# Graph attention on one core: turning probability blocks and adding edge masks as two halves of 64 rows, with both masks of pairs 1 and 2 laid by ScalarE

## Chip, cores and metric

The kernel runs on one core of a Trainium2 chip. The metric is the device time of one execution in microseconds (us), the median of several. A single profiled execution gives the rows shown below; times in rows are counted from the start of its span.

## What is computed

One layer over 1250 nodes with 512 features and 8 heads of 64. The part that this change touches is attention over the edges of a graph: for each edge a score, a softmax over all edges of a node and head, and a weighted sum of values.

```python
scores = jnp.einsum('ehd,ehd->eh', q[origin], k[destination]) * SCALE
ws = scores * edge_weights                      # 41250 edges x 8 heads
seg_max = jax.ops.segment_max(ws, origin, num_segments=N)
e = jnp.exp(ws - seg_max[origin])
denom = jax.ops.segment_sum(e, origin, num_segments=N)
att = e / (denom[origin] + 1e-16)
values = jax.ops.segment_sum(att[:, :, None] * v[destination], origin, num_segments=N)
```

Ahead of it stand two normalisations, the projections, and a linear attention over the same rows; behind it an output projection, a residual, a normalisation and some bit arithmetic on 48 columns. None of these is changed.

## The kernel before

The edges are scattered into a dense table of 1250 rows by 1360 columns (nodes, and 110 extra columns for edges that occur twice), and attention is then computed densely: an empty cell gets a penalty of -BIG, so that its exponential is zero. The rows are cut into 10 tiles of 128 nodes (the last has 98), the columns into three groups of 512, 512 and 336. A **tile** w (0 to 29) is one row tile in one group: 0 to 9 are group 0, 10 to 19 group 1, 20 to 29 group 2. Its eight heads are four **pairs** 0 to 3, and `u = 4 w + pair` numbers the pairs through the program; `hh` is 0 or 1, the head in its pair. A **step** d (0 to 59) handles two pairs: an even step (`q == 0`) pairs 0 and 1, an odd one pairs 2 and 3. So a tile is two steps.

For each head of a step, in this order over the engines:

- TensorE, `scores(d)` (L1319): two heads of a pair at once, one in array rows 0 to 63 and one in rows 64 to 127, since a head has 64 features. Each f32 product is two instructions of 512 columns, so a step has 8.
- The mask. `mask(w)` on VectorE (L1728) makes the penalty `pen` of a tile once, in bf16, in the odd step of the tile before. It is then put into the bank of PSUM in one of two ways: either ScalarE copies it there before the scores, which then add to it (`lay_mask`, L920; the head is "laid"), or TensorE adds it behind the scores as a product with the identity `identb` (L1326, 128x128). The table `OVER_MASK` says which heads of a group are laid.
- VectorE, `weighted` (L1841): multiplies scores and edge weights, takes the running maximum, and writes `ws`; `shift_of` (L1855) negates the maximum.
- ScalarE, `exps` (L912): the exponential in place, two instructions for a pair.
- TensorE, `transposes(d - 1)` (L1342): turns each head's 128x512 into four blocks 128x128 in one bank. ScalarE (`probs`, L927) or VectorE (`odd_probs`, L1862) copies the bank to SBUF.
- TensorE, `values` (L1364): the products with V, 64 columns of the array a head.

Each engine has a fixed order written out as code. That of TensorE in step d is `scores(d)`, the mask additions of step d, `transposes(d - 1)`, `values` of step d - 2. Seven banks are used as a ring in the order of the list `USES`: a bank is free for its next use when its reader has counted up its semaphore. In an even step the last of the four banks that `transposes(d - 1)` writes, that of pair 3's second head, is the bank that `scores(d)` used for pair 0's first head, so `free` waits until VectorE has read that one.

ScalarE in an odd step copies turned blocks, then does

```python
for u, hh in lay_order(d):
    if hh == 0:
        lay_mask(u, hh)
if late:
    pairs(2 * d - 1)
exps(2 * d)
for u, hh in lay_order(d):
    if hh == 1:
        lay_mask(u, hh)
exps(2 * d + 1)
```

where `lay_order(d)` lists the laid heads of step d + 1, here pairs 0 and 1 of the next tile. `lay_mask` waits for that tile's `mask` and for the bank. VectorE in an odd step does `weighted` four times, then `mask(w + 1)`, in group 1 `rescaled(w - 1)` (L1887), a shift and the copies. In an even step it starts with `weighted` of pair 0. `scores` waits for both laid heads of a pair ahead of that pair.

Of the kernel before, what the change touches and what calls it, by code (L numbers as in the profile page):

```python
# [15 lines left out]
P = 128  # L16
NT = 10
# [28 lines left out]
GROUPS = ((0, 512), (512, 512), (1024, COLS - 1024))  # L46
# [5 lines left out]
ND = NU // 2  # L52
NB = 7
ODD_ON_ACT = ((2,), (1, 2), ())
OVER_MASK = (((3, 1), (1, 1), (2, 0), (2, 1)), ((3, 1), (1, 1), (2, 0), (2, 1)), ((2, 0), (2, 1), (3, 1), (0, 0), (1, 0)))
FIN = ((0, 8), (8, 2))


def rows_of(t):
    return LAST if t == NT - 1 else P  # L60
# [7 lines left out]
def blocks(g):  # L68

    d0, n = GROUPS[g]  # L70
    return ((0, P, 8), (P, LAST, 9), (N - d0, X, None)) if g == 2 else tuple((i * P, P, d0 // P + i) for i in range(4))
# [7 lines left out]
def laid(u, hh):  # L79

    return u > 5 and (u % 4, hh) in OVER_MASK[u // 4 // NT] and not partly_written(USE_OF["s", u, hh] - NB)


def partly_written(r):

    return USES[r][0] == "t" and rows_of(USES[r][1] // 4 % NT) < P
# [12 lines left out]
def four(d):  # L99

    return [(2 * d + i // 2, i % 2) for i in range(4)]


def emptied(k):
# [63 lines left out]
def gps_layer(nc, x, src, dst, w_edge, ln_g, ln_b, Wq, bq, Wk, bk, Wv, bv, W1, b1, W2, b2,  # L168
# [3 lines left out]
    with ctx:  # L172
# [5 lines left out]
        def sem(name):  # L178
            return ctx.enter_context(nc.semaphore(name))
# [20 lines left out]
        ident = sb("ident", [P, P])  # L200
        identb = sb("identb", [P, P], BF16)
# [41 lines left out]
        def ar(a, n, parts=P):  # L243
            return AR[0:parts, a:a + n]
# [61 lines left out]
        ws = [sets, sets, [tight[0], tight[1], sets[2], tight[2]]]  # L306
        KVx = [ar(10240 + 1024 * i, 1024) for i in range(3)]
        pen = [ar(14192 + 256 * i, 256).bitcast(BF16) for i in range(2)]
# [106 lines left out]
        s_s = [sem(f"scores_ready{i}") for i in range(4)]  # L415
        s_bk = [sem(f"bank_read{i}") for i in range(NB)]
        s_nm = sem("shift_ready")
        s_exp = sem("exp_ready")
        s_t = sem("probs_transposed")
        s_pv = sem("values_summed")  # L420
        s_vfa = sem("first_values_kept")
        s_vfd = sem("values_merged")
# [52 lines left out]
        def use(what):  # L475

            return bank[USE_OF[what] % NB][:, :]
# [11 lines left out]
        def free(eng, what):  # L489

            r = USE_OF[what]
            if r >= NB:
                eng.wait_ge(s_bk[r % NB], r // NB)
# [518 lines left out]
        def _(pe):  # L1012
            mm = nc.tensor.matmul
# [103 lines left out]
            for m in range(KC):  # L1117
                b = proj(("w1t", m))
                for i in range(KC):
                    last = nc.tensor.transpose(b[:, i * P:(i + 1) * P], sW1[:, i, m * P:(m + 1) * P], ident[:, :])  # L1120
# [15 lines left out]
            for m in range(KC):  # L1136
                last = mm(b[:, m:m + 1], ball[:, m * P:(m + 1) * P], fourth[:, 0:1], start=True, stop=True)
# [101 lines left out]
            for k in range(KC):  # L1239
                last = nc.tensor.transpose(b[:, k * P:(k + 1) * P], kvBD[:, k, :], ident[:, :])  # L1240
# [59 lines left out]
            def scores(d):  # L1300
                w, q = d // 2, d % 2
                g, c = w // NT, w % NT
                d0, n = GROUPS[g]
                if g == 2 and q == 0:
                    gone(pe, ("l", w))
                for p in (2 * q, 2 * q + 1):
                    u = 4 * w + p
                    over = [laid(u, hh) for hh in range(2)]
                    bs = [use(("s", u, hh)) for hh in range(2)]
                    qs = [QT[64 * hh:64 * hh + 64, p, c * P:(c + 1) * P] for hh in range(2)]  # L1310
                    if u in (1, 2):
                        banks_left((2 * u - 2, 2 * u - 1))
                    for hh in range(2):
                        if over[hh]:
                            pe.wait_ge(s_laid, LAID_OF[u, hh] + 1)
                        else:
                            free(pe, ("s", u, hh))
                    for hh in range(2):
                        last = mm(bs[hh][:, 0:n], qs[hh], KT[64 * hh:64 * hh + 64, p, d0:d0 + n], start=not over[hh], stop=over[hh], skip_group_check=over[hh])  # L1319
                        if over[hh]:  # L1320
                            last.then_inc(s_s[2 * (p % 2) + hh], 1)
                if q == 0:
                    pe.wait_ge(s_pen, w + 1)
                for i, (u, hh) in enumerate(four(d)):
                    if not laid(u, hh):
                        mm(use(("s", u, hh))[:, 0:n], identb[:, :], pen[w % 2][:, 0:n], start=False, stop=True).then_inc(s_s[i], 1)  # L1326

            def last_mix():
                r = rows_of(NT - 1)
# [3 lines left out]
                last.then_inc(s_ly, 1)  # L1333

            def transposes(d):
                g, r = d // 2 // NT, rows_of(d // 2 % NT)
                for u, hh in four(d):
                    pe.wait_ge(s_exp, 2 * u + hh + 1)
                    free(pe, ("t", u, hh))
                    bl = blocks(g)  # L1340
                    for i, (a, rws, _) in enumerate(bl):
                        last = mm(use(("t", u, hh))[0:rws, i * P:i * P + r], ws[g][u % 4][hh][0:r, a:a + rws], ident[0:r, 0:r],  # L1342
                                  start=(i == 0), stop=(i == len(bl) - 1), is_transpose=True)
                    last.then_inc(s_t, 1)
# [55 lines left out]
            for d in range(ND + 4):  # L1400
                w, q = d // 2, d % 2
# [666 lines left out]
```

## Time and profile before

| | |
|---|---|
| median of 3 runs | 1080.33 us (1077.6 to 1081.13) |
| profiled execution, its own time | 1079.38 us |
| its span | 1077.5 us |
| TensorE busy (MATMUL) | 737.6 us, 68% of the span |
| VectorE busy | 544.0 us, 50% |
| ScalarE busy | 397.4 us, 37% |
| attention stage, three groups | about 673 to 1069 us of the span |

The span is the time from the first to the last instruction of the program; the execution's own time is 1.88 us more. Busy shares over the whole span are low because the first 500 us prepare the table, wait for the scatter and normalise; in the attention stage all three compute engines are mostly busy. MATMUL durations overlap one another since matmuls are pipelined: the distance between starts, not the duration, is what one costs.

### The profile page before, as it was taken

The page shows a single profiled execution, that of the slowest core. Times are in us where ns is not written, and L with a number is a line of the kernel's source. Part 1 is how long each engine was busy: PE and PEld are TensorE (multiplying, and loading weights), DVE is VectorE, ACT ScalarE, POOL GpSimd, SP SyncE. Part 2 cuts the span into 40 slices and gives each one's busy share as a digit, 9 for nine tenths or more (in the row PEclk, how much of TensorE's full clock was granted, in tenths as well). Part 3 has the DMA queues.
Part 4 walks back from the last instruction along what each step waited for, and adds up shares of the span by engine and source line. Part 5 has one row for each costly group of instructions (what it writes and reads, how often), then busy time and mean ns, then how long its engine had stood idle before and what let it go on. Part 6 is the DMA issues. An engine that isn't in the chain of part 4 may idle for free.

```text
span 1077.5 us, 13741 instructions
## 1 busy us (share of the span) xinstructions
PE 737.6 (68%) x4498; PEld 436.4 (41%) x4537; DVE 544.0 (50%) x1269; ACT 397.4 (37%) x943; POOL 392.7 (36%) x401
## 2 busy tenths in 40 slices
PE   7744510494332211115999999999999999999996
PEld 4321100241001011003544454576766667767773
DVE  4601400482000110200532473888889999999998
ACT  2300001020000000001313020689989998877773
POOL 2677577477777776562572000000000000000002
PEclk9956655696555555556999999999999999999998
DMA  9788866536500000002400021444444444443323
GB/s 323 270 292 302 281 239 212 179 112 219 193 23 3 23 3 22 22 3 79 153 2 1 1 79 78 149 185 172 158 157 157 161 164 167 150 140 137 137 69 96
DMA packets 71115, 143.12 MB, mean 133 GB/s; under 512 B 22565, under 2 KB 57137, under 8 KB 67079
## 3 DMA queue, kind: packets, MB, share of 16 engines
q1 hardware_dynamic: 48884, 120.06, 30.7%
q10 hardware_dynamic: 8464, 15.84, 4.2%
q0 software_dynamic: 13696, 6.33, 3.1%
q8 instruction: 38, 0.62, 0.2%
q14 instruction: 33, 0.27, 0.1%
HBM read 77.47 MB, written 64.80 MB: 132 GB/s over the span
## 4 chain that ended last, share of the span: by engine, by line
PE 50%; another core or an unknown queue 20%; issue 20%; DVE 6%; ACT 2%; DMA 2%; ACTq 1%; DVEq 0%; POOLq 0%
PE bank L1092 11%; PE bank L1319 9%; PE bank L1364 7%; PE bank L1342 7%; PE bank L1077 6%; PE bank L1388 3%; PE bank L1326 2%; DVE AR L1841 1%; PE bank L1370 1%; DMA AR<-in_L_mix_bp_dram 1%; DVE QMN L1451 1%; DVE QMN L1450 1%; PE bank L1112 1%; DMA AR<-kv_rows,xd 1%
## 5 line engine op out<-in xcount | busy, mean ns | idle before, releaser
L630 POOL DMA_INDIRECT w_tab<-pay,idx x330 | 326.5, 989 | 160.0 <-issue 116.1
L1077 PE MATMUL bank<-AR 128*128 128x512 f32 (+1 forms) x288 | 130.9, 587 | 122.7 <-issue 102.8
L705 POOL DMA_INDIRECT AR<-kv_rows,xd x10 | 10.5, 1051 | 445.4 <-PE bank L1364 331.6
L1092 PE MATMUL bank<-AR 128*128 128x512 f32 (+1 forms) x240 | 128.6, 666 | 62.4 <-issue 62.4
L1077 PEld LDWEIGHTS bank<-AR 128*128 128x128 f32 x288 | 62.3, 222 | 180.3 <-issue 156.3
L1541 DVE TENSOR_TENSOR V<-bank,bias_row 128x512 f32<-128x512 f32 (+1 forms) x10 | 6.9, 691 | 250.0 <-remote 153.5
L912 ACT ACTIVATE AR<-AR,nmx 128x512 f32<-128x512 f32 (+1 forms) x180 | 118.5, 662 | 20.6 <-DVE nmx L1855 20.5
L1841 DVE CUSTOM_DVE_ANT_0 AR<-bank,AR,MX 128x512 f32<-128x512 f32 (+1 forms) x120 | 114.9, 986 | 8.6 <-remote 7.6
L1319 PE MATMUL bank<-KT,QT 64*128 64x512 f32 (+1 forms) x480 | 108.6, 568 | 4.0 <-ACT bank L920 3.7
L1092 PEld LDWEIGHTS bank<-AR 128*128 128x128 f32 (+1 forms) x240 | 48.3, 205 | 133.5 <-issue 133.0
L1364 PE MATMUL bank<-AR,V 128*64 128x128 f32 (+1 forms) x1520 | 101.9, 274 | 0.2 <-ACT AR L927 0.2
L1364 PEld LDWEIGHTS bank<-AR,V 128*64 128x64 f32 x1520 | 85.0, 137 | 10.1 <-issue 9.0
L927 ACT ACTIVATE AR<-bank 128x512 f32<-128x512 f32 (+3 forms) x150 | 79.6, 553 | 25.4 <-PE bank L1342 24.9
L1342 PE MATMUL bank<-ident,AR 128*128 128x128 f32 (+4 forms) x660 | 81.0, 270 | 2.0 <-issue 1.4
L1342 PEld LDWEIGHTS bank<-ident,AR 128*128 128x128 f32 (+4 forms) x660 | 72.7, 139 | 3.1 <-issue 1.5
L1841 DVE CUSTOM_DVE_ANT_0 AR<-bank,AR 128x512 f32<-128x512 f32 x60 | 63.7, 1089 | 10.6 <-remote 10.5
L920 ACT ACTIVATE bank<-AR 128x512 f32<-128x512 bf16 (+1 forms) x122 | 63.7, 541 | 13.4 <-DVE MX L1841 11.2
L801 ACT ACTIVATE KT<-bank,kbias 128x512 f32<-128x512 f32 (+1 forms) x12 | 7.2, 608 | 161.6 <-remote 137.4
L781 ACT ACTIVATE AR<-bank 128x512 f32<-128x512 f32 (+1 forms) x10 | 6.0, 596 | 145.9 <-issue 89.1
L1319 PEld LDWEIGHTS bank<-KT,QT 64*128 64x128 f32 x480 | 42.0, 185 | 39.1 <-issue 18.8
L1070 PE MATMUL bank<-AR,fourth 128*128 128x512 f32 x2 | 2.1, 1141 | 61.8 <-DVE AR L1524 61.8
L1862 DVE COPY AR<-bank 128x512 f32<-128x512 f32 (+3 forms) x70 | 42.9, 636 | 0.3 <-issue 0.3
(272 smaller groups left out, 1013.2 us busy)
## 6 DMA issues: line engine op xcount, KB each, us to landing
w_tab<-ztile SPq DMA_DIRECT2D x20, 2280.0 KB
AR<-w_tab SPq DMA_DIRECT2D x20, 2048.0 KB, 7.4
AR<-w_tab SPq DMA_DIRECT2D x10, 1344.0 KB, 6.2
w_tab<-ztile SPq DMA_DIRECT2D x3, 1800.0 KB
w_tab<-pay,idx POOLq DMA_INDIRECT x330
w_tab<-ztile SPq DMA_DIRECT2D x2, 1700.0 KB
kv_rows<-AR ACTq DMA_DIRECT2D x9, 256.0 KB
kv_rows<-V ACTq DMA_DIRECT2D x9, 256.0 KB
```

The costliest lines, as they stand in the source:

```text
L630: pool.indirect_dma_start(out=w_tab, out_offset=bass.IndirectOffsetOnAxis(ap=idx[:, k, j:j + 1], axis=0), in_=pay[:, k % RING, j, :], in_o ...
L912: act.activation(ws[g][u % 4][hh][:, 0:n], ws[g][u % 4][hh][:, 0:n], ACT.Exp, bias=nmx[:, u % 4, hh:hh + 1], accum_out=DG[g][:, c, 2 * p + ...
L920: act.activation(use(("s", u, hh))[:, 0:n], pen[w % 2][:, 0:n], ACT.Copy).then_inc(s_laid, 1)
L927: act.activation(turned(PT[g][u % 4][hh], u), turned(use(("t", u, hh)), u), ACT.Copy).then_inc(read(("t", u, hh)), 1)
L1077: last = mm(b[:, 0:n], w[:, k, m * P:(m + 1) * P], src_t(k), start=(k == 0), stop=(k == KC - 1))
L1092: last = mm(b[0:r, :], src_t(k)[:, 0:r], w[:, k, :], start=(k == 0), stop=(k == KC - 1))
L1319: last = mm(bs[hh][:, 0:n], qs[hh], KT[64 * hh:64 * hh + 64, p, d0:d0 + n], start=not over[hh], stop=over[hh], skip_group_check=over[hh])
L1342: last = mm(use(("t", u, hh))[0:rws, i * P:i * P + r], ws[g][u % 4][hh][0:r, a:a + rws], ident[0:r, 0:r], start=(i == 0), stop=(i == len(b ...
L1364: last = mm(bank[7][64 * hh:64 * hh + 64, p * P:p * P + r], v, PT[g][u % 4][hh][0:rws, i * P:i * P + r], start=(i == 0), stop=(i == len(bl ...
L1388: last = mm(use(("y", w)), (tb_last if w == NW - 1 else tb)[:, k * P:(k + 1) * P], W12[:, k, :], start=(k == 0), stop=(k == KC - 1))
L1841: v.tensor_tensor_reduce(out=ws[g][u % 4][hh][:, 0:n], in0=use(("s", u, hh))[:, 0:n], in1=Wt[w % 2][:, 0:n, h], scale=1.0, scalar=MX[g - 1 ...
L1862: v.tensor_copy(turned(PT[g][u % 4][1], u), turned(use(("t", u, 1)), u)).then_inc(read(("t", u, 1)), 1)
```

## The change

Three things change together.

1. `OVER_MASK` of groups 0 and 1 lays pairs 1 and 2 with both heads. Before, pair 2 with both heads and the second heads of pairs 1 and 3. The count stays four heads a tile.
2. Where `in_halves(d)` holds, `transposes(d)` becomes `halves(d)`: every 128x128 block is turned as two products of 64 rows (`ws` rows 0 to 63 and 64 to 127, with a 64x64 piece of the identity), the two heads of a pair in different halves of the array rows at a time, as in `scores`. `in_halves` is true for steps 1 to 17 and 20, and for the odd steps 21 to 37: 27 in all. Both heads of a pair are then finished by its second half only.
3. The masks that TensorE adds in the steps behind these are added as halves too: the first halves behind the scores, the second halves inside `halves`, behind the first half of the first pair's blocks. The scores of such a head are signalled ready (`s_s`) by the second half.

Two semaphores order halves that write the same bank.

```diff
-OVER_MASK = (((3, 1), (1, 1), (2, 0), (2, 1)), ((3, 1), (1, 1), (2, 0), (2, 1)), ((2, 0), (2, 1), (3, 1), (0, 0), (1, 0)))
+OVER_MASK = (((1, 0), (1, 1), (2, 0), (2, 1)), ((1, 0), (1, 1), (2, 0), (2, 1)), ((2, 0), (2, 1), (3, 1), (0, 0), (1, 0)))
+def in_halves(d):
+
+    t, q = divmod(d + 1, 2)
+    return d > 0 and t < 2 * NT and (q == 0 or t <= NT) and rows_of(d // 2 % NT) == P
@@ scores
                 if q == 0:
                     pe.wait_ge(s_pen, w + 1)
+                for u in by_halves(d):
+                    masks(u, 0)
                 for i, (u, hh) in enumerate(four(d)):
-                    if not laid(u, hh):
+                    if not laid(u, hh) and u not in by_halves(d):
+            def by_halves(d):
+
+                return [u for u in (2 * d, 2 * d + 1) if in_halves(d - 1) and not laid(u, 0) and not laid(u, 1)]
+
+            def masks(u, half):
+
+                w, n = u // 4, GROUPS[u // 4 // NT][1]
+                for hh in range(2):
+                    a = (hh + half) % 2
+                    q64 = slice(64 * a, 64 * a + 64)
+                    last = mm(use(("s", u, hh))[:, 0:n], identb[q64, :], pen[w % 2][q64, 0:n], start=False, stop=(half == 1))
+                    if half:
+                        last.then_inc(s_s[2 * (u % 2) + hh], 1)
+                    else:
+                        mh.inc(last)
+
+            def turn_halves(u, half):
+
+                g = u // 4 // NT
+                bl = blocks(g)
+                if half == 0:
+                    for hh in range(2):
+                        pe.wait_ge(s_exp, 2 * u + hh + 1)
+                        free(pe, ("t", u, hh))
+                for i, (a, rws, _) in enumerate(bl):
+                    for hh in range(2):
+                        j = (hh + half) % 2
+                        q64 = slice(64 * j, 64 * j + 64)
+                        last = mm(use(("t", u, hh))[0:rws, i * P + 64 * j:i * P + 64 * j + 64], ws[g][u % 4][hh][q64, a:a + rws], ident[q64, q64],
+                                  start=(half == 0 and i == 0), stop=(half == 1 and i == len(bl) - 1), is_transpose=True)
...
+            def halves(d):
+
+                first = [0, 0]
+                for i in range(2):
+                    turn_halves(2 * d + i, 0)
+                    first[i] = th.n
+                    if i == 0:
+                        pe.wait_ge(s_mh, mh.n)
+                        for u in by_halves(d + 1):
+                            masks(u, 1)
+                for i in range(2):
+                    pe.wait_ge(s_th, first[i])
+                    turn_halves(2 * d + i, 1)
@@ transposes
+                if in_halves(d):
+                    halves(d)
+                    return
```

ScalarE's program in an odd step of group 0, before: two copies of turned blocks, the exponentials of pair 2 (`bias_row`), one mask (bank<-AR, L920), the exponentials of pair 3.

```order
L927 ACTIVATE AR<-bank 128x512 [waits values_summed,probs_transposed] x2
L912 ACTIVATE bias_row,DG<-bias_row,nmx 128x512 [waits shift_ready]
L912 ACTIVATE bias_row,DG<-bias_row,nmx 128x512
L920 ACTIVATE bank<-AR 128x512 [waits bank_read4,mask_ready]
L912 ACTIVATE AR,DG<-AR,nmx 128x512 [waits shift_ready]
```

The same place in the changed kernel (its line numbers are 8 higher on this engine; L928 is the mask, L920 the exponentials):

```order
L935 ACTIVATE AR<-bank 128x512 [waits values_summed,probs_transposed] x2
L928 ACTIVATE bank<-AR 128x512 [waits bank_read3,mask_ready]
L920 ACTIVATE bias_row,DG<-bias_row,nmx 128x512 [waits shift_ready]
L920 ACTIVATE bias_row,DG<-bias_row,nmx 128x512
L928 ACTIVATE bank<-AR 128x512 [waits bank_read4,mask_ready]
L920 ACTIVATE AR,DG<-AR,nmx 128x512 [waits shift_ready]
```

A mask that waits for `mask_ready` now stands ahead of pair 2's exponentials, and the second mask behind them.

TensorE's program in the even step of group 0 that follows, before: scores of pair 0, scores of pair 1, three mask additions, the turned blocks head by head.

```order
L1319 MATMUL bank<-KT,QT 128x512 [waits bank_read0,bank_read6]
L1319 MATMUL bank<-KT,QT 128x512
L1319 MATMUL bank<-KT,QT 128x512 [waits mask_laid,bank_read1]
L1319 MATMUL bank<-KT,QT 128x512
L1326 MATMUL bank<-AR,identb 128x512 [waits mask_ready]
L1326 MATMUL bank<-AR,identb 128x512 x2
L1342 MATMUL bank<-ident,bias_row 128x128 [waits bank_read3,exp_ready]
L1342 MATMUL bank<-ident,bias_row 128x128 x3
L1342 MATMUL bank<-ident,bias_row 128x128 [waits bank_read4,exp_ready]
```

The same place in the changed kernel (L1327 scores, L1350 mask halves, L1368 halves of blocks; `bias_row` is pair 2, `AR` pair 3):

```order
L1327 MATMUL bank<-KT,QT 128x512 [waits bank_read0,bank_read6]
L1327 MATMUL bank<-KT,QT 128x512
L1327 MATMUL bank<-KT,QT 128x512 [waits mask_laid]
L1327 MATMUL bank<-KT,QT 128x512
L1350 MATMUL bank<-AR,identb 128x512 [waits mask_ready]
L1350 MATMUL bank<-AR,identb 128x512
L1368 MATMUL bank<-ident,bias_row 128x64 [waits exp_ready,bank_read4,bank_read3]
L1368 MATMUL bank<-ident,bias_row 128x64 x7
L1350 MATMUL bank<-AR,identb 128x512 [waits first_halves_masked]
L1350 MATMUL bank<-AR,identb 128x512
L1368 MATMUL bank<-ident,AR 128x64 [waits exp_ready,bank_read6,bank_read5]
L1368 MATMUL bank<-ident,AR 128x64 x7
```

The second halves of pair 0's masks have moved behind eight half blocks, and the next instruction behind them waits for `bank_read6`, the count of the bank that held pair 0's first head.

## Rows read from the trace of the kernel before

**Rows 1.** Windows: length, busy us (count) of PE, PEld, DVE, ACT, POOL, clock, DMA.
```profile
673.00:802.00 129.00, 124.58 (x1134) 87.03 (x1153) 113.71 (x249) 108.36 (x256) 2.13 (x2) 1.00 0.46 170
802.00:931.00 129.00, 122.73 (x1183) 90.23 (x1202) 121.14 (x281) 116.39 (x274) 0.00 (x0) 1.00 0.41 154
```
**Rows 2.** Chain that ended last, one tile of group 0: start, us, what.
```profile
773.12 0.16 issue
...
773.88 1.75 PE bank L1342 x16
775.62 1.90 PE bank L1364 x32
```
**Rows 3.** Timeline, group 0, odd step's end into even: start, us, engine, line [idle <-releaser].
```profile
761.22 1.10 DVE L1841 CUSTOM_DVE_ANT_0 AR<-bank,AR 128x512 f32<-128x512 f32 x1 [1.11 <-remote]
...
769.70 0.72 ACT L912 ACTIVATE bias_row<-bias_row,nmx 128x512 f32<-128x512 f32 x1 [0.24 <-DVE nmx L1855]
...
770.58 0.63 DVE L1728 TENSOR_SCALAR AR<-AR 128x512 bf16<-128x512 f32 x1
...
771.25 0.60 ACT L920 ACTIVATE bank<-AR 128x512 f32<-128x512 bf16 x1
771.78 0.71 ACT L912 ACTIVATE AR<-AR,nmx 128x512 f32<-128x512 f32 x1
771.96 0.33 PEld L1319 LDWEIGHTS bank<-KT,QT 64*128 64x128 f32 x4 [0.58 <-issue]
...
772.49 0.70 ACT L912 ACTIVATE AR<-AR,nmx 128x512 f32<-128x512 f32 x1
773.05 0.33 PEld L1326 LDWEIGHTS bank<-AR,identb 128*128 128x128 bf16 x3 [0.76 <-issue]
...
773.59 1.11 DVE L1841 CUSTOM_DVE_ANT_0 AR<-bank,AR 128x512 f32<-128x512 f32 x1 [1.11 <-remote]
```
**Rows 4.** Timeline, group 0, the even step that follows.
```profile
773.71 1.04 PE L1342 MATMUL bank<-ident,bias_row 128*128 128x128 f32 x8
774.35 1.09 ACT L927 ACTIVATE AR<-bank 128x512 f32<-128x512 f32 x2 [0.58 <-PE bank L1342]
...
775.55 1.97 PE L1364 MATMUL bank<-AR,V 128*64 128x128 f32 x32
776.73 1.09 DVE L1841 CUSTOM_DVE_ANT_0 AR<-bank,AR 128x512 f32<-128x512 f32 x1
776.84 0.60 ACT L920 ACTIVATE bank<-AR 128x512 f32<-128x512 bf16 x1 [0.40 <-DVE MX L1841]
777.55 0.33 PEld L1319 LDWEIGHTS bank<-KT,QT 64*128 64x128 f32 x4 [0.27 <-ACT bank L920]
778.09 0.22 PEld L1319 LDWEIGHTS bank<-KT,QT 64*128 64x128 f32 x2 [0.21 <-DVE MX L1841]
778.82 1.08 DVE L1841 CUSTOM_DVE_ANT_0 bias_row<-bank,AR 128x512 f32<-128x512 f32 x1 [0.32 <-PE bank L1319]
```
**Rows 5.** Timeline (first row) and scores in a view of their line: lengths of runs on TensorE.
```profile
767.35 1.91 PE L1342 MATMUL bank<-ident,AR 128*128 128x128 f32 x16 [0.16 <-issue]
L1319 PE MATMUL bank<-KT,QT x42: 589/589/693, 758.7 to 789.9; 64*128 64x512 f32 x42
```
**Rows 6.** Timeline, group 1, the same places.
```profile
846.63 0.63 DVE L1728 TENSOR_SCALAR AR<-AR 128x512 bf16<-128x512 f32 x1
847.19 0.67 DVE L1887 TENSOR_TENSOR QMN<-bank,QMN 128x512 f32<-128x512 f32 x1
...
848.15 0.33 PEld L1319 LDWEIGHTS bank<-KT,QT 64*128 64x128 f32 x4 [0.56 <-DVE QMN L1887]
849.80 1.17 DVE L1841 CUSTOM_DVE_ANT_0 AR<-bank,AR,MX 128x512 f32<-128x512 f32 x1 [0.61 <-remote]
853.94 0.33 PEld L1319 LDWEIGHTS bank<-KT,QT 64*128 64x128 f32 x4 [0.48 <-ACT bank L920]
855.25 1.15 DVE L1841 CUSTOM_DVE_ANT_0 bias_row<-bank,AR,MX 128x512 f32<-128x512 f32 x1
```

More of the change, by code:

```diff
@@ L419, in gps_layer @@
         s_t = sem("probs_transposed")
+        s_th = sem("first_halves_transposed")
+        s_mh = sem("first_halves_masked")
         s_pv = sem("values_summed")
@@ L1323, in scores @@
                     pe.wait_ge(s_pen, w + 1)
+                for u in by_halves(d):
+                    masks(u, 0)
                 for i, (u, hh) in enumerate(four(d)):
-                    if not laid(u, hh):
+                    if not laid(u, hh) and u not in by_halves(d):
                         mm(use(("s", u, hh))[:, 0:n], identb[:, :], pen[w % 2][:, 0:n], start=False, stop=True).then_inc(s_s[i], 1)
+            mh, th = Count(pe, s_mh), Count(pe, s_th)
+            def by_halves(d):
+                return [u for u in (2 * d, 2 * d + 1) if in_halves(d - 1) and not laid(u, 0) and not laid(u, 1)]
@@ new lines, in turn_halves @@
+            def turn_halves(u, half):
[11 more added lines that the diff above has]
+                                  start=(half == 0 and i == 0), stop=(half == 1 and i == len(bl) - 1), is_transpose=True)
+                        if i == len(bl) - 1:
+                            if half:
+                                last.then_inc(s_t, 1)
+                            else:
+                                th.inc(last)
```

## The prediction, made before the changed kernel was run

> **What bounds the kernel now.** I first read the windows of groups 0 and 1 [rows 1]. TensorE is busy for 124.6 and 122.7 us of 129, at a granted clock of 1.00, VectorE for 113.7 and 121.1. TensorE looks like the bound, but VectorE is so near that a closed loop through both could bind as well. The chain that ended last says TensorE too: in a tile it goes from one TensorE run to the next, with an "issue" of 0.16 us ahead of the mask additions [rows 2]. A chain that follows one engine hides a second one of nearly the same length, so I read the timeline by places.
>
> I look at one event in each tile: W, when VectorE starts `weighted` of pair 0. Two stretches lead from one W to the next. M is the end of `mask(w + 1)`, VectorE's last work before it can use the next tile. In group 0 [rows 3]: the mask ends at M = 770.58 + 0.63 = 771.21. ScalarE lays a mask at 771.25. TensorE loads pair 1's scores at 771.96, which is 0.11 after that mask's end (771.25 + 0.60). The mask additions start at 773.05. VectorE starts at W = 773.59, after 1.11 us of idle. So M to W is 2.38, and every link waits for the one ahead of it. The second stretch is W to W', the next step's first `weighted`, 778.82 [rows 4]: 5.23. It too ends with a wait, of 0.32, for scores that wait for a mask laid by ScalarE. The rest, from W' to the next M, is VectorE's own work, 4.76: a tile is 12.37, from the W of the tile before, 761.22, to this one [rows 3]. So the loop VectorE, ScalarE, TensorE, VectorE is already closed without slack, beside a TensorE that is nearly full. Whatever lengthens it lengthens the tile.
>
> **What the change saves.** The scores already use array rows 0 to 63 and 64 to 127, the masks and turned blocks all 128. Between them stands 0.16 of "issue" [rows 2], once a step. Halves make scores, masks and blocks alike, so 27 steps can save 0.16 each, 4.3 us. The mask additions are no dearer: three at (773.71 - 773.05) / 3 = 0.22 [rows 3, 4] and one in the odd step, against two pairs of halves in each, four times 0.22 either way. The half blocks are not in the trace. A full block costs (1.91 - 0.27) / 15 = 0.109, from a run of 16 [rows 5], the 0.27 being the last one's own duration (the run of eight of 1.04 in rows 4 gives the same pitch, as the difference is (1.91 - 1.04) / 8). There are 16 blocks a step before and 16 pairs of half blocks now. A pair streams half as many columns but loads as many weight columns, in both row halves at once. The scores show such a load: their first instruction lasts 0.693 against 0.589 [rows 5], so the exposed load of two row halves together is 0.104, about one block's pitch. I take 0.109 a pair: no gain. Bounds: 0.055 if only the streamed columns counted, 0.218 if the two loads came one behind the other. The value products run two instructions and two loads in (1.97 - 0.27) / 15.5 = 0.11 [rows 4], so the issue of four instructions is no further limit.
>
> The Trainium skill, "TensorE: Matmul & The Clock Gate", Part 3, says that weight loads overlap running matmuls only where the row groups differ. By it a pair would cost its load and then its half stream, 0.109 + 0.055 = 0.16 by this case's rows. The full blocks, whose loads and matmuls share all rows, show 0.109 for both together, so the trace speaks against it; I keep it as a rival.
>
> **What it adds: ScalarE's order.** In the odd step, the mask of pair 1's first head now stands ahead of pair 2's exponentials. It needs `mask(w + 1)`. Before, these exponentials started at 769.70, 1.5 us before M [rows 3]; now they start behind it. And the second head's mask, for which pair 1's scores wait on TensorE, stands behind the exponentials. From M: 0.04 to the first mask, 0.53 to the exponentials (771.25 to 771.78), 0.71 twice (771.78 to 772.49), 0.60 for the second mask, 0.11 to TensorE's load: M + 2.70, where it was M + 0.75.
>
> **TensorE and back.** From that load to the first mask halves: 1.09 before, less the 0.16, so 0.93. Then 0.22 for the first halves, 0.44 for four pairs of half blocks of pair 2, and, from the second halves' start to VectorE, the 0.54 of now (773.05 to 773.59). M to W becomes 2.70 + 0.93 + 0.22 + 0.44 + 0.54 = 4.83: **2.45 more**.
>
> **W to W'.** The instruction behind the second mask halves turns pair 3 and needs the bank that VectorE reads from W on. It starts at W + 1.09 (VectorE's instruction) + 0.27 (776.73 + 1.09 to the load at 778.09 [rows 4]) = W + 1.36. Then 0.10 of load, 12 pairs 1.31, 0.10 to the values (773.71 to 775.55 less 16 times 0.109), 1.90 for them [rows 2]: the next scores at W + 4.77. On ScalarE, pair 2's blocks are complete only after two of the three remaining parts, at W + 1.46 + 0.87; 0.20 later (774.35 less 773.71 + 0.44) it copies twice (0.53 each, half the 1.09 for two), lays twice (0.53 and 0.60), and 0.11 later the scores load: W + 4.83. It was 777.55 - 773.59 = 3.96: **0.87 more**, and VectorE follows by its 1.27 as now. A tile of group 0 grows by 3.32.
>
> **Group 1** [rows 6]. The bank of the first mask is freed by `rescaled`, which ends at 847.86, 0.60 behind M = 847.26. By the same links the load comes at 847.86 + 0.04 + 0.53 + 1.42 + 0.60 + 0.11 = 850.56, 2.41 behind 848.15; from it to W 2.13 against 1.65. Together 2.89. W to W': the load at W + 4.83 + 0.07 (an instruction of 1.16), then 1.27, so 6.17 against 5.45: 0.72. A tile grows by 3.61. Odd steps keep whole blocks there.
>
> **The sum.** Tiles 2 to 9: 8 x 3.32 = 26.6. Tiles 11 to 19: 9 x 3.61 = 32.5, less 0.6 since the first has no `rescaled`. Tile 1 lays no masks of pair 1, so only the halves cost it: 0.66 less 0.16 and the 0.87, 1.4. Tile 10 has whole blocks and, by the rule about partly written banks, one mask: nothing. Group 2 is untouched. +59.9. Of the 4.3 us saved, what lies on the loop is in the 0.93; the rest lies where TensorE now waits. Profiled execution 1079.4 + 59.9 = 1139.3; the median lies 0.95 above it, so **1140**.
>
> **Rivals.**
> 1. *Faster: TensorE alone is the bound*, as the chain says. Then 27 drains of 0.16, perhaps 0.10 of load each: 1073 to 1076. It decides if ScalarE's first mask finds `mask(w + 1)` done when pair 2's shift is, some 1.5 us earlier than in rows 3. VectorE's order is unchanged, so I see no way. 0.05.
> 2. *Only M to W grows*; the wait for pair 0's bank or the late copies are hidden. 8 x 2.45 + 9 x 2.89 = 46: 1125. Against it: both TensorE's and ScalarE's path give 4.8. 0.12.
> 3. *Half blocks cost 0.16 a pair*: 16 pairs of a tile lie on the loop, 17 x 16 x 0.055 = 15: 1155. Loads one behind the other, 0.218: 30, so 1170, more if TensorE fills up. 0.12 for the first, 0.06 for the second.
> 4. *No difference*: the drains pay for a loop that has slack I don't see. 1080. 0.02.
>
> My forecast has 0.63. Range 1115 to 1165: rival 2 and the first of rival 3, and the bounds of the half block's price (17 x 16 x 0.054 = 15 below 1140 if it is cheap, with some rest for latencies taken from single rows). The likeliest case's own range is 1128 to 1152. About 3 us (0.3%) is what a measurement tells from no change: faster 0.05, same 0.02, slower 0.93.
>
> **What the changed profile would show.** Right: in odd steps ScalarE idles until `mask(w + 1)` ends, lays, then does pair 2's exponentials; TensorE's load of pair 1's scores waits some 2 us for a ScalarE mask; VectorE idles some 3.5 us ahead of pair 0; TensorE waits about 1.6 us for VectorE behind the second mask halves in even steps; group 0 tiles of 15.7, group 1 of 16.6; no 0.16 between scores and masks. Wrong: tiles of 12.4 with ScalarE waiting nowhere (rival 1), runs of half blocks with another pitch than 0.109 (rival 3). The granted clock is also open: TensorE will idle about a quarter of the time. In the rows it ran at 1.00 with 97% busy; if it fell to 0.5 in these gaps, all would be slower than my range.

## The result, and the profile after

| | median of 4 runs | range | profiled span | instructions |
|---|---|---|---|---|
| before | 1080.73 us | 1077.6 to 1083.22 | 1077.5 us | 13741 |
| changed | 1138.99 us | 1136.55 to 1139.51 | 1137.3 us | 14744 |

The changed kernel is slower: the ratio is 1.0536, with a 95% interval of 1.0505 to 1.0568. The forecast of 1140 us was hit, but errors of both signs stand behind it and cancel. Attention in groups 0 and 1, from step 2's scores to the first scores of group 2, took 241.96 us before (684.12 to 926.08) and takes 299.89 now (686.00 to 985.89): 57.9 of the 59.8 us by which the span grew.

These are windows of the changed kernel, columns as in rows 1: group 0 of attention, one tile of group 1, the next tile of group 1, and both groups together.

```profile
686.00:824.58 138.58, 108.05 (x1413) 74.00 (x1414) 104.32 (x229) 102.96 (x247) 0.00 (x0) 1.00 0.40 153
841.90:857.86 15.96, 12.25 (x141) 8.69 (x139) 11.21 (x23) 10.67 (x27) 0.00 (x0) 1.00 0.36 133
857.86:875.92 18.06, 14.48 (x137) 10.66 (x138) 13.35 (x34) 12.69 (x31) 0.00 (x0) 0.81 0.32 117
686.00:985.89 299.89, 235.35 (x2726) 164.44 (x2736) 220.37 (x495) 213.57 (x506) 0.00 (x0) 0.94 0.35 132
```

TensorE is now busy for 78% of these stretches, against 97% in [rows 1], and no engine has taken its place: VectorE is at 73%, ScalarE at 71%. That is how a loop looks in which each engine waits for another. The third row holds something else: a granted clock of 0.81 as the mean of one tile, where its neighbour has 1.00 and is 2.1 us shorter.

The waits of 680 to 985 us (what waited, for what, us in total, times, longest):

```profile
DVE AR L1906 <- PE bank L1350: 65.1, 18, 5.0
ACT AR L935 <- PE bank L1368: 55.2, 27, 3.7
PEld bank L1327 <- ACT bank L928: 48.1, 33, 2.9
...
PE bank L1368 <- DVE MX L1906: 25.2, 18, 1.5
...
ACT bank L928 <- DVE QMN L1952: 12.7, 8, 1.6
...
ACT bank L928 <- DVE AR L1793: 9.0, 11, 2.0
```

Each line is one link of the loop, and the counts tell how often it closes: 18 times, once for each of the 18 tiles whose masks are halves (1 to 9 and 11 to 19), VectorE waits for the mask halves (L1350); as often TensorE waits, behind the second mask halves, for the bank that VectorE's `weighted` reads; 8 + 11 times ScalarE waits for `mask` or, in group 1, for `rescaled`; and ScalarE's copies (L935) wait 27 times for half blocks (L1368), once for each step that has them. In the kernel before, the wait in the place of the first line, ahead of VectorE's `weighted`, came to 18.0 us in 19 times.

The timeline of the changed kernel, group 0, the places of [rows 3, 4]:

```profile
743.17 0.63 DVE L1793 TENSOR_SCALAR AR<-AR 128x512 bf16<-128x512 f32 x1
743.84 0.60 ACT L928 ACTIVATE bank<-AR 128x512 f32<-128x512 bf16 x1 [0.77 <-DVE AR L1793]
744.37 0.71 ACT L920 ACTIVATE bias_row<-bias_row,nmx 128x512 f32<-128x512 f32 x1
...
745.78 0.58 ACT L928 ACTIVATE bank<-AR 128x512 f32<-128x512 bf16 x1
746.48 0.33 PEld L1327 LDWEIGHTS bank<-KT,QT 64*128 64x128 f32 x4 [2.13 <-ACT bank L928]
...
747.44 0.41 PE L1350 MATMUL bank<-AR,identb 64*128 64x512 bf16 x2
747.65 0.44 PE L1368 MATMUL bank<-ident,bias_row 64*128 64x64 f32 x8
...
747.91 0.40 PE L1350 MATMUL bank<-AR,identb 64*128 64x512 bf16 x2
748.46 1.07 DVE L1906 CUSTOM_DVE_ANT_0 AR<-bank,AR 128x512 f32<-128x512 f32 x1 [3.35 <-PE bank L1350]
749.67 0.47 PE L1368 MATMUL bank<-ident,AR 64*128 64x64 f32 x8 [1.37 <-DVE MX L1906]
749.95 0.45 PE L1368 MATMUL bank<-ident,bias_row 64*128 64x64 f32 x8
750.20 0.46 PE L1368 MATMUL bank<-ident,AR 64*128 64x64 f32 x8
...
752.64 0.33 PEld L1327 LDWEIGHTS bank<-KT,QT 64*128 64x128 f32 x4 [0.32 <-ACT bank L928]
...
753.91 1.09 DVE L1906 CUSTOM_DVE_ANT_0 bias_row<-bank,AR 128x512 f32<-128x512 f32 x1 [0.59 <-PE bank L1327]
...
756.10 0.99 PE L1368 MATMUL bank<-ident,AR 64*128 64x64 f32 x24 [0.73 <-ACT AR L920]
```

Read it as a chain from M = 743.17 + 0.63 = 743.80. ScalarE's first mask starts 0.04 later, the second ends at 746.36, TensorE's load comes at 746.48, M + 2.68 (forecast 2.70). The mask halves start 0.96 behind it (747.44), while the scores still run: the 0.16 between scores and masks is gone. W is 748.46, so M to W is 4.66. From W, VectorE keeps its bank until 749.53 and TensorE goes on at 749.67. W to W' is 753.91 - 748.46 = 5.45. With 4.74 from W' to the next M a tile has 14.86 (4.66 + 5.45 + 4.74, to rounding), against 12.37.

The half blocks have a surprise in them. Sets of four pairs start at 749.95 and 750.20, so a pair costs 0.25 / 4 = 0.0625. The run of 24, whose last instruction takes 0.22 by itself, comes near: (0.99 - 0.22) / 11.5 = 0.067, with the changes from one half to the other in it.

Group 1, the places of [rows 6]:

```profile
847.62 0.62 DVE L1793 TENSOR_SCALAR AR<-AR 128x512 bf16<-128x512 f32 x1
848.16 0.68 DVE L1952 TENSOR_TENSOR QMN<-bank,QMN 128x512 f32<-128x512 f32 x1
848.93 0.60 ACT L928 ACTIVATE bank<-AR 128x512 f32<-128x512 bf16 x1 [1.59 <-DVE QMN L1952]
...
851.57 0.33 PEld L1327 LDWEIGHTS bank<-KT,QT 64*128 64x128 f32 x4 [2.79 <-ACT bank L928]
...
853.58 1.13 DVE L1906 CUSTOM_DVE_ANT_0 AR<-bank,AR,MX 128x512 f32<-128x512 f32 x1 [3.40 <-PE bank L1350]
...
859.13 1.15 DVE L1906 CUSTOM_DVE_ANT_0 bias_row<-bank,AR,MX 128x512 f32<-128x512 f32 x1 [0.16 <-DVE den L1941]
```

M to W is 853.58 - 848.24 = 5.34 (forecast 5.43), W to W' 5.55 (forecast 6.17). VectorE starts W' right behind its own work (L1941), so here this second stretch no longer has a wait for a score. A tile at full clock has 15.9 against 13.0. In six tiles of group 1 (from 834.3, 868.4, 885.5, 919.6, 953.8 and 970.8) the granted clock fell from 1.00 (2.4 GHz) to 0.5 (1.2 GHz) for 3.4 to 6.8 us. In their even steps, the stretch from pair 1's scores to the next step's scores took 8.43 us (four times) or 7.81 (twice) instead of 6.25: 4 x 2.18 + 2 x 1.56 = 11.8 us.

The whole, counted from scores to scores: tile 1 adds 1.1, tiles 2 to 9 add 19.3 (2.49 each, the last less), tile 10 adds 0.2, tiles 11 to 19 add 37.4, of which the clock is 11.8, and the stage starts 1.9 later. Together they are the 59.8 by which the span grew, to rounding.

### The profile page after: what moved, and what is told of

Its sections match the earlier page's. It is cut to its first block, busy times and chain, and to the rows that moved or that the text cites. A ratio compares the mean times of both kernels' runs of the same rounds, so it can differ in the third digit from the quotient of the medians.

```text
span 1137.3 us, 14744 instructions
## 1 busy us (share of the span) xinstructions
PE 740.4 (65%) x5013; PEld 432.7 (38%) x5025; DVE 543.4 (48%) x1269; ACT 395.0 (35%) x943; POOL 391.0 (34%) x401
## 4 chain that ended last, share of the span: by engine, by line
PE 44%; another core or an unknown queue 20%; issue 19%; DVE 9%; ACT 6%; DMA 1%; DVEq 0%; ACTq 0%; POOLq 0%
PE bank L1100 11%; PE bank L1085 7%; PE bank L1429 6%; PE bank L1327 5%; PE bank L1453 3%; DVE AR L1906 2%; PE bank L1407 2%; PE bank L1368 2%; ACT bias_row L920 2%; ACT AR L920 2%; DVE QMN L1516 1%; PE bank L1120 1%; ACT bank L928 1%; DVE QMN L1515 1%
## 5 line engine op out<-in xcount | busy, mean ns | idle before, releaser
L1327 PE MATMUL bank<-KT,QT 64*128 64x512 f32 (+1 forms) x480 | 114.9, 583 | 30.7 <-ACT bank L928 29.2
L1906 DVE CUSTOM_DVE_ANT_0 AR<-bank,AR,MX 128x512 f32<-128x512 f32 (+1 forms) x120 | 114.7, 985 | 39.7 <-PE bank L1350 37.4
L920 ACT ACTIVATE AR<-AR,nmx 128x512 f32<-128x512 f32 (+1 forms) x180 | 118.6, 667 | 20.5 <-DVE nmx L1920 20.5
L1429 PE MATMUL bank<-AR,V 128*64 128x128 f32 (+1 forms) x1520 | 106.0, 281 | 0.1
L935 ACT ACTIVATE AR<-bank 128x512 f32<-128x512 f32 (+3 forms) x150 | 79.3, 556 | 75.6 <-PE bank L1368 55.2
L1429 PEld LDWEIGHTS bank<-AR,V 128*64 128x64 f32 x1520 | 89.2, 142 | 7.6 <-issue 4.5
L1044 PE MATMUL bank<-ident,AR 128*128 128x128 f32 x40 | 8.3, 339 | 120.4 <-issue 110.5
L1906 DVE CUSTOM_DVE_ANT_0 AR<-bank,AR 128x512 f32<-128x512 f32 x60 | 63.6, 1085 | 29.4 <-PE bank L1350 27.8
L928 ACT ACTIVATE bank<-AR 128x512 f32<-128x512 bf16 (+1 forms) x122 | 62.6, 538 | 25.9 <-DVE QMN L1952 12.7
L1327 PEld LDWEIGHTS bank<-KT,QT 64*128 64x128 f32 x480 | 42.1, 187 | 69.7 <-ACT bank L928 48.3
L1575 DVE SCALAR_TENSOR_TENSOR AR<-AR,cols,QMN 128x512 f32<-128x512 f32 (+1 forms) x12 | 7.4, 661 | 114.2 <-issue 112.4
L778 ACT ACTIVATE QT<-bank,qbias 128x512 f32<-128x512 f32 (+1 forms) x12 | 6.9, 607 | 136.2 <-remote 129.2
L1044 PEld LDWEIGHTS bank<-ident,AR 128*128 128x128 f32 x40 | 5.3, 167 | 124.1 <-issue 113.5
L1368 PE MATMUL bank<-ident,AR 64*128 64x64 f32 x576 | 31.4, 239 | 31.7 <-DVE MX L1906 25.2
```

Source lines behind the costliest of these rows:

```text
L920: act.activation(ws[g][u % 4][hh][:, 0:n], ws[g][u % 4][hh][:, 0:n], ACT.Exp, bias=nmx[:, u % 4, hh:hh + 1], accum_out=DG[g][:, c, 2 * p + ...
L928: act.activation(use(("s", u, hh))[:, 0:n], pen[w % 2][:, 0:n], ACT.Copy).then_inc(s_laid, 1)
L935: act.activation(turned(PT[g][u % 4][hh], u), turned(use(("t", u, hh)), u), ACT.Copy).then_inc(read(("t", u, hh)), 1)
L1368: last = mm(use(("t", u, hh))[0:rws, i * P + 64 * j:i * P + 64 * j + 64], ws[g][u % 4][hh][q64, a:a + rws], ident[q64, q64], start=(half = ...
L1429: last = mm(bank[7][64 * hh:64 * hh + 64, p * P:p * P + r], v, PT[g][u % 4][hh][0:rws, i * P:i * P + r], start=(i == 0), stop=(i == len(bl ...
L1906: v.tensor_tensor_reduce(out=ws[g][u % 4][hh][:, 0:n], in0=use(("s", u, hh))[:, 0:n], in1=Wt[w % 2][:, 0:n, h], scale=1.0, scalar=MX[g - 1 ...
```

## The experiments

They ran on two chips, e1 to e4 on one and the others on the second. On both, the part ahead of attention takes some 370 us less than in the runs above, so that the kernel before takes 711.4 to 711.6 us. Attention takes the same time: each kernel is read by its difference to the runs of the kernel before that stood beside it, and by its tiles. Medians are of 4 runs, of 12 for e8.

| kernel | median | to before | ratio (95%) | tile, groups 0 / 1 |
|---|---|---|---|---|
| e5 the changed kernel | 767.84 | +56.2 | 1.0796 (1.0773 to 1.0819) | 14.86 / 15.9 |
| e1 new table alone | 756.62 | +45.3 | 1.063 (1.0604 to 1.0657) | 14.27 / 15.44 |
| e2 halves alone | 742.38 | +31.0 | 1.0445 (1.0421 to 1.047) | 14.45 / 14.46 |
| e3 changed, masks laid late | 739.15 | +27.8 | 1.0383 (1.036 to 1.0406) | 13.98 / 14.5 |
| e6 new table, laid late | 724.48 | +12.9 | 1.0179 (1.0159 to 1.0198) | 12.89 / 14.03 |
| e4 halves, new orders | 707.07 | -4.3 | 0.9934 (0.9916 to 0.9951) | 11.95 / 12.8 |
| e7 e4, VectorE's order as before | 705.51 | -6.1 | 0.9919 (0.9901 to 0.9937) | 11.74 / 12.7 |
| e10 e7, both masks ahead of a copy | 707.57 | -4.1 | 0.9945 (0.9926 to 0.9964) | 12.19 / 12.7 |
| e8 e4, halves in group 2 too | 709.86 | -1.8 | 0.9978 (0.9966 to 0.9989) | |
| e9 e7, halves in group 2, paired | 705.02 | -6.6 | 0.991 (0.9892 to 0.9928) | |

Tiles of group 1 are those at full clock.

**e5, the changed kernel once more**, without an edit, as the base for the rest.

> The changed kernel itself beside the kernel before, on the chip of this series, where the part ahead of the attention may take another time than in the first measurement. My theory (all of the loss is in the attention stage of groups 0 and 1): the same difference to before as in the first measurement, 56 to 62 us, whatever the total. Rival (part of it comes from ahead of the attention): another difference.

Measured +56.2, with the same tile of 14.86 in group 0. The falls of the clock came in four tiles here, 3 x 2.18 + 1.56 = 8.1 us. That is 3.7 less than in the first measurement, where the difference was +58.3.

**e1, the table alone**: the kernel before with the new `OVER_MASK` and whole blocks.

```diff
-OVER_MASK = (((3, 1), (1, 1), (2, 0), (2, 1)), ((3, 1), (1, 1), (2, 0), (2, 1)), ...
+OVER_MASK = (((1, 0), (1, 1), (2, 0), (2, 1)), ((1, 0), (1, 1), (2, 0), (2, 1)), ...
```

> The kernel before with the new table of laid heads alone; blocks and masks stay whole. My theory (ScalarE's order closes the longer part of the loop): the load of pair 1's scores moves from M + 0.75 to M + 2.70 in group 0 and by 2.41 in group 1, the step behind is unchanged, so 8 x 1.9 + 9 x 2.4 = 37 us, about 1117. Rival (the halves and their waits are what costs, the table is harmless): within 3 us of 1080.

Its timeline in group 0:

```profile
399.99 0.62 DVE L1728 TENSOR_SCALAR AR<-AR 128x512 bf16<-128x512 f32 x1
400.64 0.60 ACT L920 ACTIVATE bank<-AR 128x512 f32<-128x512 bf16 x1 [1.56 <-DVE AR L1728]
...
403.27 0.33 PEld L1319 LDWEIGHTS bank<-KT,QT 64*128 64x128 f32 x4 [2.26 <-ACT bank L920]
```

M is 400.61 and the load 403.27, M + 2.66. The tile of group 0 grew by 1.9, as expected. The rest of the +45.3 was not expected: in group 1 the granted clock fell in seven tiles, each 1.08 to 1.15 us longer for it from pair 1's scores to the next step's, 7.7 us together. So the late masks alone, with whole blocks, both make the wait and bring the falls.

**e2, the halves alone**: the changed kernel with the old table.

> The changed kernel with the old table: blocks in halves, masks in halves only for pair 0, whole for single heads. My theory: ScalarE's first mask no longer stands ahead of the exponentials, so the long wait goes; left is what the late second halves and the bank of pair 0 cost, M to W plus 0.7, W to W' plus 0.8, 17 tiles x 1.5 = 26 us, about 1106. Rival 1 (the table is all of it and half blocks at 0.062 us a pair now pay): below 1075. Rival 2 (halves are all of it): 1135 or more.

```profile
385.68 0.64 DVE L1793 TENSOR_SCALAR AR<-AR 128x512 bf16<-128x512 f32 x1
387.56 0.33 PEld L1327 LDWEIGHTS bank<-KT,QT 64*128 64x128 f32 x4 [0.72 <-issue]
...
388.87 0.10 PEld L1336 LDWEIGHTS bank<-AR,identb 128*128 128x128 bf16 x1 [0.64 <-issue]
...
390.02 1.06 DVE L1906 CUSTOM_DVE_ANT_0 AR<-bank,AR 128x512 f32<-128x512 f32 x1 [2.44 <-PE bank L1350]
...
392.96 1.64 ACT L928 ACTIVATE bank<-AR 128x512 f32<-128x512 bf16 x3
...
394.72 0.33 PEld L1327 LDWEIGHTS bank<-KT,QT 64*128 64x128 f32 x4 [0.84 <-ACT bank L928]
```

The loss is 31.0 where 26 was expected, and neither rival came. Here ScalarE's mask no longer stands ahead of the exponentials, and yet M to W is 390.02 - 386.32 = 3.70 instead of 2.38, since pair 0 is ready only behind the second mask halves. Behind the second mask halves TensorE waits 1.36 for VectorE's bank, as in the changed kernel. The next scores load at W + 4.70, when ScalarE has laid three masks in a row. With the old table one whole mask (L1336, all 128 rows) still stands between the halves, which the changed kernel doesn't have. So e1 and e2 don't add up: 45.3 + 31.0 is more than the 56.2 of both together, and neither number is the share of its part in the change.

**e3, masks of pair 1 laid late**: the changed kernel, but in groups 0 and 1 ScalarE lays both behind pair 2's exponentials.

```diff
-                        if hh == 0:
+                        if hh == 0 and w + 1 >= 2 * NT:
                             lay_mask(u, hh)
...
-                        if hh == 1:
+                        if hh == 1 or w + 1 < 2 * NT:
                             lay_mask(u, hh)
```

> The changed kernel, but in groups 0 and 1 both masks of pair 1 are laid behind pair 2's exponentials. My theory: the load of pair 1's scores comes 1.4 us earlier behind M, tiles of group 0 at 13.5 instead of 14.86, group 1 at 14.5, and no falls of the clock in group 1: about 1104. Rival (pair 0's bank is what binds, ScalarE's order is hidden behind it): within 5 us of 1139.

```profile
399.12 0.63 DVE L1793 TENSOR_SCALAR AR<-AR 128x512 bf16<-128x512 f32 x1
400.31 1.11 ACT L928 ACTIVATE bank<-AR 128x512 f32<-128x512 bf16 x2
401.54 0.33 PEld L1327 LDWEIGHTS bank<-KT,QT 64*128 64x128 f32 x4 [1.24 <-ACT bank L928]
...
403.52 1.07 DVE L1906 CUSTOM_DVE_ANT_0 AR<-bank,AR 128x512 f32<-128x512 f32 x1 [2.50 <-PE bank L1350]
404.74 0.46 PE L1368 MATMUL bank<-ident,AR 64*128 64x64 f32 x8 [1.37 <-DVE MX L1906]
```

This one exchange gives back 28.4 of the 56.2 us; 35 was expected. M to W is 3.77, with the wait for VectorE (1.37) unchanged. That is half of the matter, with the 8.1 us of the clock in it, which doesn't fall here (below). What is left, 27.8, lies in TensorE's order and the two masks in a row; this run doesn't part them. A tile of group 0 is 0.5 longer than expected since ScalarE's exponentials end only at 400.31, M + 0.56.

**e6, the same with whole blocks**: e1 with the edit of e3.

> The kernel before with the new table, and both masks of pair 1 laid behind pair 2's exponentials. My theory: nearly all of the 45 us of the table alone came from the mask that stood ahead of the exponentials; left is one mask more between M and pair 1's scores, 0.53 us in 17 tiles, 9 us above before. Rival (two masks of one pair in a row are the cost, wherever they stand): 30 us or more above before.

Tiles of 12.89 in group 0 are 0.5 over before, as expected, those of group 1 1.03, which makes 12.9 instead of 9. The first mask waits there for the bank that `rescaled` frees (8 times, 1.8 us in all), and the second stands behind it, so that pair 1's scores load at 473.85, M + 1.93. So the table costs 12.9 us where its masks are laid late, and the other 32.4 of e1's 45.3 come from one mask that waits ahead of ready exponentials, the clock's 7.7 among them.

**The clock** in windows of 465 to 600 us, within group 1. That of e5, the changed kernel:

```profile
465.00:600.00 135.00, 107.27 (x1104) 75.53 (x1104) 98.67 (x224) 92.83 (x217) 43.83 (x37) 0.91 0.38 133
```

That of e3, with the masks laid late:

```profile
465.00:600.00 135.00, 115.89 (x1307) 84.85 (x1315) 116.61 (x275) 109.14 (x263) 42.90 (x35) 1.00 0.43 146
```

And that of e1, the new table with whole blocks:

```profile
465.00:600.00 135.00, 114.77 (x985) 82.34 (x999) 102.99 (x235) 98.66 (x228) 42.75 (x35) 0.92 0.38 128
```

The clock (0.91, 1.00, 0.92) fell in the two kernels in which ScalarE's mask waits ahead of the exponentials, with half blocks and with whole ones, and not in e3. In the other runs' attention stages, e6 with its whole blocks among them, it stayed at 1.00 as well.

**e4, the halves with orders of their own.** If the loop is the cause, the halves should gain once it is opened in three places: TensorE signals pair 0 early, ScalarE lays late, and VectorE makes the mask one instruction earlier. In the even step TensorE now does pair 0's scores and first mask halves, pair 2's first half blocks, pair 0's second mask halves, and only then pair 1's scores. ScalarE lays one mask of pair 2 behind the copy of pair 3's blocks, pair 1's second mask ahead of its first (`lay_order`), and both as late as in e3. Pair 2's second halves come ahead of pair 3's first ones.

```diff
@@ lay_order, odd steps
-        order = ((1, 0), (0, 0), (0, 1), (1, 1))
+        order = ((1, 0), (0, 0), (0, 1), (1, 1)) if d // 2 + 1 >= 2 * NT else ((1, 1), (1, 0))
@@ scores, in even steps d > 2 with halves (early)
+                    if early(d) and p == 0:
+                        pe.wait_ge(s_pen, w + 1)
+                        masks(u, 0)
+                        turn_halves(2 * d - 2, 0)
+                        firsts[d - 1] = th.n
+                        pe.wait_ge(s_mh, mh.n)
+                        masks(u, 1)
@@ VectorE, odd step
+                    if w + 1 < 2 * NT:
+                        mask(w + 1)
                     weighted(2 * d + 1, 1)
@@ ScalarE, even step
-                    for u, hh in lay_order(d):
+                    lays = lay_order(d)
+                    now = lays if late or len(lays) != 2 else lays[:1]
+                    for u, hh in now:
                         lay_mask(u, hh)
                     if d >= 1:
                         pairs(2 * d - 1)
+                    for u, hh in lays[len(now):]:
+                        lay_mask(u, hh)
...
```

> A version that keeps the halves and takes both waits off the loop: both masks of pair 1 behind the exponentials; in even steps pair 0's scores, first mask halves, pair 2's first half blocks, second mask halves, only then pair 1's scores; pair 2's second halves ahead of pair 3's first; the mask made one instruction earlier on VectorE; one of two masks of pair 2 laid behind pair 3's copy. My theory: VectorE's 1.1 us of idle ahead of pair 0 mostly goes in group 0, up to 0.6 in group 1: 1066 to 1074. Rival (the half blocks' gain on TensorE is worthless because TensorE never was the bound): 1080 or more.

4.3 us faster than before, so 60.5 better than e5: the side was right, but the gain is smaller than the 6 to 14 us expected.

**e7, without the mask's move on VectorE.**

> The fast version without the move of the mask on VectorE. My theory: TensorE's order in even steps is what gave the gain; M comes 0.5 us later than in the fast version and pair 0's mask halves wait for it a little: 1 to 4 us slower than the fast version, near before. Rival (the early mask is the whole gain, since it shortens M to W): 15 us or more above before.

A miss: it is 1.6 us faster, not slower, and tiles of group 0 show it (11.74 against 11.95), though the two intervals in the table overlap. That the mask, one instruction earlier, holds up pair 3's last `weighted` and its shift would explain this; no run tells it apart. Its timeline in group 0, to be held against that of the changed kernel:

```profile
399.55 0.63 DVE L1810 TENSOR_SCALAR AR<-AR 128x512 bf16<-128x512 f32 x1
...
400.85 0.38 PE L1368 MATMUL bank<-AR,identb 64*128 64x512 bf16 x2
...
401.32 0.39 PE L1368 MATMUL bank<-AR,identb 64*128 64x512 bf16 x2
...
401.55 1.02 PE L1331 MATMUL bank<-KT,QT 64*128 64x512 f32 x4
401.85 1.09 DVE L1923 CUSTOM_DVE_ANT_0 AR<-bank,AR 128x512 f32<-128x512 f32 x1 [0.41 <-PE bank L1368]
...
403.10 0.99 PE L1386 MATMUL bank<-ident,AR 64*128 64x64 f32 x16 [0.29 <-DVE MX L1923]
```

M is 400.18 and W 401.85: M to W is 1.67, against 4.66 in the changed kernel and 2.38 before. The wait for VectorE's bank has shrunk from 1.37 to 0.29, since pair 1's scores now fill it. From 380 to 417 us TensorE is busy for 35.71 of 37 us here, and for 28.50 in e5. So the kernel with half blocks beats the one before once these waits are short. How much of that is the half blocks' own doing isn't shown: whole blocks with the new orders were not run. Nor was TensorE's order run alone. Of the 33.9 us between e3 and e7, the exchange that e10 takes back is worth 2.1; the rest is TensorE's order together with that of pair 1's two masks, not parted by any run.

**e10, both masks of pair 2 ahead of pair 3's copy**: e7 with `now = lays`.

> The version without the mask's move, and ScalarE lays both masks of pair 2 ahead of pair 3's copy again, as in the changed kernel. My theory (the second of these masks waits for VectorE, and what stands behind it is late by half a microsecond): 2 to 6 us slower than with the swap. Rival (ScalarE has the room): the same within 1 us.

2.1 us slower than e7, within what was expected, with tiles of 12.19 against 11.74.

**e8, half blocks in group 2 as well**: e4 with `in_halves` true there too, while masks stay whole.

> The fast version with half blocks in group 2 as well, masks there whole. Half blocks cost 0.062 a pair against 0.109 a block, 12 a step, less one change of array mode of 0.16: 0.4 us a step, 18 steps, 7 us. My theory (TensorE is the bound in group 2, where VectorE has 5% idle): 5 to 7 us below the fast version, 1.4% below before. Rival (the later end of a pair's blocks is not hidden there): no better than the fast version.

My reason fell: it is 2.8 us slower than e4, by 0.26 a step in group 2 (5.20 and 8.87 against 4.94 and 8.61). TensorE's instructions of one step in e8 show one part of it:

```profile
618.20 0.39 PE L1386 MATMUL bank<-ident,bias_row 64*128 64x64 f32 x6
...
618.77 0.39 PE L1386 MATMUL bank<-ident,bias_row 64*128 64x64 f32 x6 [0.18 <-PE bank L1386]
```

With no mask halves between them, the first pair's second halves wait 0.18 for the completion of their own first halves, once in each of the 17 steps, 3.1 us in all.

**e9, first halves of both pairs, then second halves**, in group 2, on the base of e7.

```diff
+                if d >= 4 * NT:
+                    first = [0, 0]
+                    for i in range(2):
+                        turn_halves(2 * d + i, 0)
+                        first[i] = th.n
+                    for i in range(2):
+                        pe.wait_ge(s_th, first[i])
+                        turn_halves(2 * d + i, 1)
+                    return
```

> The version without the mask's move, and half blocks in group 2 in the order first halves of both pairs, then second halves of both. In the run before, group 2's steps were 0.26 us longer than with whole blocks, and TensorE waited for its own first halves. My theory (that wait is the reason): steps of group 2 fall 0.3 to 0.4 us below whole blocks, 6 us in all, about 699, 1.7% below before. Rival (half blocks of this shape are no cheaper, or VectorE has no room): steps stay at 4.94 and 8.61 or above, 705 or more.

Half right. The wait is gone (24 half blocks in one run of 1.04 us), and the odd steps of group 2 are 0.33 shorter, 8.28. But the even ones are 0.30 longer, 5.25, so a tile stays at 13.5. Two rows of an even step of e9, whose scores start at 612.17, show where:

```profile
614.95 0.39 PE L1386 MATMUL bank<-ident,AR 64*128 64x64 f32 x6 [0.23 <-DVE MX L1932]
...
615.55 0.49 ACT L935 ACTIVATE AR<-bank 128x384 f32<-128x384 f32 x1 [1.09 <-PE bank L1386]
```

The same copy in an even step of e4, whose scores start at 616.55:

```profile
619.15 0.49 ACT L935 ACTIVATE AR<-bank 128x384 f32<-128x384 f32 x1 [1.01 <-PE bank L1424]
```

TensorE waits 0.23 for the bank that VectorE reads. Pair 2's blocks are complete only behind pair 3's first halves, so ScalarE's copy starts 3.38 behind the scores instead of 2.60, the mask behind it is late too, and the next step's scores wait for it: 7 times, 2.6 us, where e4 has 4 times and 0.7. That is again the loop, and the rival of e8, that the later end of a pair's blocks isn't hidden in group 2. At 705.02 it can't be told from e7's 705.51.

## Why the prediction was right, and where it wasn't

- *The loop VectorE, ScalarE, TensorE, VectorE bounds the kernel*: shown. The places named ahead (ScalarE's first mask, TensorE's load, pair 0 on VectorE, the wait behind the second mask halves) all wait, and e3 and e4 shorten the kernel by taking single links out. Rival 1, TensorE alone as the bound, and rival 4 are out by the 1138.99 us.
- *ScalarE's order, M to the load + 2.70*: right at 2.68 in the changed kernel and 2.66 in e1.
- *W to W' grows by 0.87, in group 1 by 0.72*: this step failed. It grew by 0.22 and 0.10. The wait for pair 0's bank came (1.37), but what it delays ends little later than before. In group 0, ScalarE's copies and masks end last, as forecast, but 0.65 earlier: eight pairs of half blocks save 8 x 0.047 = 0.37 there, and TensorE goes on at W + 1.21 (749.67) where I had W + 1.46, because I took 0.27 + 0.10 for a hand-over from VectorE that took 0.14. In group 1, W' starts behind VectorE's own work.
- *"I take 0.109 a pair"*: this failed too, and is part of the same. A pair of half blocks costs 0.062, near the lower bound of 0.055. The exposed load in the scores, 0.104, was the wrong row to price it by: it is more than a whole pair took. In all a tile is 0.82 shorter than forecast in group 0 (0.17 of it in M to W, for four pairs) and 0.72 in group 1: 8 x 0.82 + 9 x 0.72 = 13 us less. The pitch explains some two thirds of the 0.82, since 12 pairs of a tile lie on the path that ends last, not 16.
- *Rival 2, only M to W grows, 1125 us*: nearly what happened. M to W grew by 2.28 and 2.80; without the clock's 11.8 us the changed kernel would be at some 1127 us.
- *Rival 3, 0.16 a pair*, is out by the same rows. The Trainium skill, "TensorE: Matmul & The Clock Gate", Part 3, says that weight loads overlap running products only where the row groups differ, and the two heads of a pair alternate between row groups. I had applied its rule as if both loads had to be done ahead of both streams. The 0.062 fits the rule if each load runs under the other head's product, but doesn't prove it, and the 0.109 for load and stream of a whole block, on the same rows, still speaks against it. Which of load and stream sets the 0.062 no run here shows.
- *Granted clock left open*: it fell, and cost 11.8 us in the first measurement and 8.1 in e5. I had the case as one that would go beyond my range, and put no term for it into the sum. A partial fall was the one that came.
- The 13 too much and the 11.8 too little, with the 1.9 us by which the stage starts later, cancel. The loop and its longer part, M to W, were foreseen; that the total came within 1 us was luck.
- *Tile 10 and group 2 unchanged, tile 1 +1.4*: tile 1 cost 1.1, and from group 2's first scores to the end both kernels take 151.4 us.

Open: what exactly brings the clock down; why e7 beats e4; what whole blocks would do in e7's orders.

## What to carry to other kernels

An engine that is 97% busy can still be part of a closed loop with another: follow one event from tile to tile through the timeline, and price a change by the links of that loop, not by the busiest engine's work. In an engine with a fixed order, never put an instruction that waits for something late ahead of ones that are ready: one mask ahead of two exponentials cost 28 to 32 us, some 8 of them by the clock. A kernel slower with a new form of work says little on that form until the order around it fits: the same halves were 56 us slower than the kernel before and, with other orders, 6 us faster (0.9919). To say that the new form itself gives the gain, the old form has to be run in the new orders too, which was not done here.

## What the runs showed of the hardware

- Pairs of turned half blocks (64 rows each, in the two halves of the array) run at 0.062 us a pair, whole blocks at 0.109: the same data in little more than half of the time.
- TensorE's granted clock fell to 0.5 in group 1 of the changed kernel, where TensorE has a gap of 1.96 to 2.05 us ahead of pair 1's scores in each tile, and stayed at 1.00 in group 0, where that gap is 1.31 to 1.33. It fell in six of these nine tiles only, so the gap alone doesn't decide. With whole blocks (e1) the same place has 1.97 to 2.16 us in group 1, with falls in seven tiles of nine, and 1.46 to 1.50 in group 0, with none.
- In e8, TensorE's second halves that wait for its own first halves just ahead of them start 0.18 us after these have ended.
